# Later attentions: the first half's transposes of probabilities stand behind the queries' projection, and VectorE scales the rotation in front of their copy

## The reference

```python
def _layer(x, wqkv, qs, ksc, wo, lg, lb, w1, b1, w2, b2):
    h = shift_token(x)
    q, k, v = jnp.split(h @ wqkv, 3, axis=-1)          # 8 heads of 64
    q = l2norm(q) * qs
    k = l2norm(k) * ksc
    q, k = rotary_xpos(q, k)                           # q * cos * scale + rotate_half(q) * sin * scale
    o = local_attention(q, k, v)                       # windows of 128 queries see 256 keys
    x = x + o @ wo
    ...                                                # shift, layer norm, gated MLP, residual
for l in range(DEPTH):                                 # DEPTH = 2
    x = _layer(x, ...)
```

## Time and profile before

| | |
|---|---|
| median of 3 runs | 1796.6 us (1796.27 to 1797.61) |
| the profiled execution | 1796.15 us, of which 1794.4 us from the first to the last instruction |
| mean granted TensorE clock | 0.993 |
| busy: PE, DVE, ACT, POOL | 96%, 83%, 67%, 59% |
| chain that ended last: PE, DVE, ACT | 83%, 9%, 3% |

### The profile page before, as it was taken

The page is one execution under the profiler, slowest core; times in us unless marked ns, Lnnn a source line. Parts: engine busy times, 40 slices in busy tenths (PEclk is TensorE's granted clock), DMA queues, the critical chain, the costliest instruction groups (busy, mean ns, idle before and its releaser), DMA issues.

```text
span 1794.4 us, 43797 instructions
## 1 busy us (share of the span) xinstructions
PE 1730.8 (96%) x15424; PEld 1495.9 (83%) x15424; DVE 1495.9 (83%) x3797; ACT 1205.5 (67%) x3118; POOL 1066.2 (59%) x1030
## 2 busy tenths in 40 slices
PE   6999999999999999999999999989999999999997
PEld 4777777779998788888887888878888888888886
DVE  6999888858888898988987778789898888967776
ACT  6999999854445687877876344358787877743332
POOL 3666455534434778787774455377878777734343
PEclk9999999999999999999999999999999999999999
DMA  3111211022322111111112434321111111131221
GB/s 107 37 37 37 72 38 31 26 104 73 101 67 100 52 44 54 41 54 45 50 43 70 147 102 129 100 103 41 50 45 55 41 54 46 32 98 59 82 82 36
DMA packets 139813, 116.04 MB, mean 65 GB/s; under 512 B 10584, under 2 KB 138848, under 8 KB 138848
## 3 DMA queue, kind: packets, MB, share of 16 engines
q1 hardware_dynamic: 139616, 113.53, 20.4%
HBM read 75.74 MB, written 37.75 MB: 63 GB/s over the span
## 4 chain that ended last, share of the span: by engine, by line
PE 83%; DVE 9%; ACT 3%; issue 3%; POOL 1%; DMA 0%; SPq 0%; DVEq 0%; POOLq 0%; ACTq 0%
PE psum L567 17%; PE psum L569 17%; PE psum L568 17%; PE psum L908 6%; PE psum L876 5%; PE psum L889 5%; PE psum L682 3%; PE psum L664 3%; PE psum L850 3%; ACT a_probs L1720 2%; PE psum L922 2%; PE psum L617 1%; DVE a_neg_max L1211 1%; DVE psum L1209 1%; PE psum L654 1%
## 5 line engine op out<-in xcount | busy, mean ns | idle before, releaser
L1838 ACT ACTIVATE b_probs<-masked,neg_max 128x256 f32<-128x256 f32 (+1 forms) x512 | 250.1, 490 | 125.8 <-DVE neg_max L1345 125.8
L567 PE MATMUL psum<-wa_hi,b_h_hi 128*128 128x512 f32 (+1 forms) x576 | 232.6, 404 | 8.5 <-DVE wa_lo L1138 3.6
L1345 DVE CUSTOM_DVE_ANT_0 masked<-psum,mask 128x256 f32<-128x256 f32 (+1 forms) x512 | 177.3, 412 | 75.9 <-PE psum L876 75.9
L569 PE MATMUL psum<-wa_hi,b_h_lo 128*128 128x512 f32 (+1 forms) x576 | 213.4, 371 | 0.0
L568 PE MATMUL psum<-wa_lo,b_h_hi 128*128 128x512 f32 (+1 forms) x576 | 212.9, 370 | 0.0
L567 PE MATMUL psum<-g_h_hi,wm_hi 128*128 128x512 f32 (+1 forms) x480 | 190.4, 397 | 3.2 <-POOL g_h_lo L2107 1.6
L2056 POOL TENSOR_TENSOR g_in<-g_in,minus_half 128x16 f32<-128x16 f32 x64 | 188.2, 2940 | 4.5 <-DVE g_in L1297 4.5
L569 PE MATMUL psum<-g_h_hi,wm_lo 128*128 128x512 f32 (+1 forms) x480 | 189.2, 394 | 0.0
L568 PE MATMUL psum<-g_h_lo,wm_hi 128*128 128x512 f32 (+1 forms) x480 | 189.1, 394 | 0.0
L1460 POOL TENSOR_TENSOR g_in<-g_z,g_in 128x512 f32<-128x512 f32 x62 | 79.8, 1287 | 144.0 <-DVE g_in L1291 138.8
L1932 ACT ACTIVATE gate<-psum,vec_b 128x512 f32<-128x512 f32 x96 | 66.0, 688 | 146.7 <-PE psum L569 146.6
(11 more groups left out here) (168 smaller groups left out, 5613.1 us busy)
## 6 DMA issues: line engine op xcount, KB each, us to landing
x_mid<-y_out SPq DMA_DIRECT2D x96, 128.0 KB, 1.7
rope_in<-in_rope SPq DMA_DIRECT2D x64, 128.0 KB, 2.2
x_res<-x_state SPq DMA_DIRECT2D x64, 128.0 KB, 2.2
g_in<-x_mid SPq DMA_DIRECT2D x32, 256.0 KB, 3.6
g_old<-x_state SPq DMA_DIRECT2D x16, 512.0 KB, 4.0
out_x<-g_fin SPq DMA_DIRECT2D x15, 512.0 KB, 2.9
w_raw<-in_w_mlp_b SPq DMA_DIRECT2D x2, 2154.0 KB, 8.9
x_in<-in_x SPq DMA_DIRECT2D x32, 128.0 KB, 2.3
```

Source lines behind the costliest of these rows:

```text
L567: nc.tensor.matmul(out, a_hi, b_hi, start=first, stop=False)
L569: return nc.tensor.matmul(out, a_lo, b_hi, start=False, stop=last)
L1345: ins = nc.vector.tensor_tensor_reduce(out[:, at], src[:, at], (mask if now else mask0)[:, at], -1.0, BIG, ALU.add, ALU.min, neg_max[:, r, ...
L1838: ins = nc.scalar.activation(out, src, ACT.Exp, bias=neg_max[:, r, k:k + 1], scale=-1.0, accum_out=row_sum[:, n % 2, 4 * r + k:4 * r + k + 1])
```

## The change

In the loop of TensorE the transposes of the first half's probabilities move from in front of `project_q` to behind `transpose_x`, for every step that has them (at step 0 they stood there already). In the loop of VectorE `scale_rotated(s + 1)` moves in front of `copy_probs(s, 0)`. No instruction is added or removed.

```diff
@@ pe_attention
                 if b_chunk(s + 2) and s + 2 > 1:
                     project_k(s + 2)
-                if b_chunk(s) and s > 0:
-                    transpose_probs(s, 0)
                 if b_chunk(s + 2) and s + 2 > 1:
                     project_q(s + 2)
                 if b_chunk(s + 3) and s + 3 > 2:
                     transpose_x(s + 3)
-                if s == 0:
+                if b_chunk(s):
                     transpose_probs(s, 0)
@@ dve_attention
+                if b_chunk(s + 1) and s + 1 > 1:
+                    scale_rotated(s + 1)
                 if b_chunk(s):
                     copy_probs(s, 0)
-                if b_chunk(s + 1) and s + 1 > 1:
-                    scale_rotated(s + 1)
```

## The result

The changed kernel takes 1820.4 us (median of 4 runs, 1816.5 to 1821.6) against 1797.1 us for the kernel before on the same chip: the ratio is 1.013, with a 95% interval of 1.0117 to 1.0142. The forecast was 1819.8. The profiled execution took 1819.78 us against the 1819.3 that the sum had given for it, and its span is 23.6 us longer than before.

What follows compares the result with a forecast made beforehand. TensorE carries 83% of the chain, but VectorE's room in front of `h_low` was taken as 0.04 us. Longer steps sum to 23.2 us on 1796.15, 1819.3; with 0.45 for the median 1819.8 us, range 1810 to 1824.

Steps and rivals of the forecast that it cites:

- TensorE's sum: TensorE's work per step stays 12.57 us; first half's transposes start at 7.03 for 5.42, rotated parts' at 8.77.
- the saved change between products and transposes: Rival: on TensorE each of 56 steps could be 0.08 us shorter, 1791.0 us in all; chance 0.03.
- the fall of the clock: Rival: 26 transposes in a row drop TensorE to 1.2 GHz, 2.8 us more a step, near 1975 us; chance 0.02.
- An ordinary step, 12.94: Step without weight split: VectorE's first copy waits for transposes until 8.10, `h_low` ends at 11.27; 0.37 us over 12.57.
- The idle stretch of VectorE: VectorE would idle 0.3 to 0.5 us in front of the first copy in an ordinary step.
- A split step, 13.29: Step with a weight split on GpSimd: `tables` holds VectorE's scalings until 8.53, copy at 8.45; 0.64 us over 12.65.
- The room of VectorE, 0.04: VectorE can be only 0.04 us later in front of `h_low`; beyond it the step ends 1.67 us after `h_low`.
- The sum: Both attentions: 36 ordinary steps by 0.37, 13 split by 0.64, step 15 0.36, partly filled steps 1.2; together 23.2 us.
- the ten partly filled steps: Steps 1, 16, 17, 29, 30 of both attentions: each between -0.37 and +0.64, +0.12 us on average, 1.2 us for ten.
- TensorE's idle stretch in front of `project_v`: TensorE would idle about 0.3 us in front of `project_v` in every step.
- What was to become late next: Keys' rotated part, ready at 7.9 (8.53 in split steps) before TensorE wants it at 8.77; cover holds by 0.2 us.

Runs made afterwards that it cites:

- The spare instruction: Kernel before with one added VectorE sum over 128x512 into an unused tile, in front of the reciprocal in steps 2 to 28: 1822.6 us, ratio 1.0158.

## Why the prediction was right

- **TensorE's sum.** Right: transposes at 7.03, rotated parts' at 8.78, nothing else moved. The transposes, 26 in a row, keep 0.109 us each ((921.54 - 919.79) / 16, over the 16 of the probabilities), and the granted clock is 1.00 over both attentions, so neither the saved change between products and transposes nor the fall of the clock came about: the rotated parts' transposes still start at 8.78 for 8.77. The rule of the Trainium skill that was weighed there ("TensorE: Matmul & The Clock Gate", Part 4: transposes do not count as busy) has no effect that this trace shows.
- **An ordinary step, 12.94.** Measured 12.94 to 12.96. Copy at 8.10, `h_low` done at 11.28 for 11.27, next scores 1.67 behind. The idle stretch of VectorE is 0.21 where 0.3 was forecast; the scalings' record overlaps the rest. The parts are shown apart by experiments: 0.07 from VectorE's order, and 0.30 more with the late transposes, 0.22 of it when they move past the two token transposes.
- **A split step, 13.29.** Measured 13.24 to 13.29. The scalings end 1.16 behind `tables`, the very figure taken from the earlier trace rows; in all 50 full steps of the changed kernel it is 1.14 to 1.16. By the Trainium skill's rule ("SBUF — State Buffer", section "Who interferes with whom") read to the letter it would have been 1.28; the measurement decides for the shorter hold. That `tables` is the cause was shown by cutting it: 0.32 us of the 0.62 went. The other 0.30 stayed because the late transposes then hold the copy at 8.10, as in ordinary steps: each cause covers a part of the other.
- **The room of VectorE, 0.04.** The spare instruction gave 0.05. This number and the 1.67 us from `h_low` to the next scores, both read from one odd step of the trace before, carry the forecast together with the hold by `tables`. In step 15 it was GpSimd's L1460 that came late (9.54 for 9.25 in the same step of the first attention) and held the clamp; for the reading of the room this makes no difference.
- **The sum.** Forecast 23.2 us, measured 12.30 + 12.00 = 24.3 in the two attentions. The term that was mis-sized is that of the ten partly filled steps: 1.2 forecast, 1.93 measured (steps 1 of both attentions +0.48 and +0.18, 16 +0.19 and +0.20, 17 +0.73 and +0.72, 29 none, 30 -0.29 and -0.28). Step 17 has a weight split and took 13.27 like the others, but was shorter to begin with (12.54), and so lies above the +0.64 that was named as an upper bound. The remaining 50 steps gave 22.4 for 22.0. Outside the attentions the two traces differ by -0.8 us (start +0.3, end -1.1); the change does not reach there, and this is no part of its effect. That the forecast of 1819.8 lies within 0.6 us of the median is therefore partly luck: 1.1 us too little in the attentions stands against 0.8 us less outside, and the four runs themselves lie 5.1 us apart.
- **TensorE's idle stretch in front of `project_v`.** Forecast 0.3 in every step; the weight load of step 26 waits 0.29. `project_v` starts 0.26 later and takes 0.12 longer from its start to the next scores (1.61 for 1.49, by the rows above and the earlier trace rows), which adds up to the step's 0.38.
- **What was to become late next.** The rotated keys are ready at 7.89 and 8.51, and TensorE takes them up at 8.78, so that cover held.

Open: single steps are 0.3 us longer than their neighbours, step 28 of the first attention (12.88 before, 13.21 after) and step 15 of the second (12.93 and 13.55). With the clamp moved, in either kernel, both are gone. In the kernel before, step 28 loses its time between the clamp and the reciprocal (0.33 us), and step 15 by GpSimd's late L1460 (0.29 us). What starts either was not looked for.

## What to carry to other kernels

On an engine that works in order, find the instruction that another engine waits for and measure the room in front of it, from a step in which something happened to be late, before moving anything ahead of it: a busy share of 83% hid a room of 0.05 us. Moving work "behind" something costs what the in-order engine then waits, beyond its room: the last 0.22 us of it were paid one for one. And putting another instruction into the gap helps only if that one is ready and not held up itself. A tiny instruction that another engine can hold up belongs where nothing is awaited behind it, but its new neighbour on the other engine has to be looked at too, and so has the timetable of that engine: with shorter steps its own work comes later in the step.

## What the runs showed of the hardware

- A pair of VectorE instructions that read two SBUF inputs and started during GpSimd's `tables` ended at a fixed distance behind it, however long it had been held: 1.14 to 1.16 us in ordinary and split steps (1.82, 1.51 and 1.39 us long), for 1.28 us of its own. A single one ended 0.55 us behind GpSimd's L1136 (rows of step 7 with the clamp moved in the changed kernel), and 0.56 in the earlier trace rows.
- Not every GpSimd instruction holds VectorE up so: VectorE's first instruction of the rotation took 0.69 us in the middle of the power in step 26 of the kernel before (904.74, while the power ran from 903.35 to 906.26).
- The smallest instruction suffered most in proportion. The clamp, 128x16 and 0.17 us, took 0.28, 1.05 and 1.21 us, ending 0.03 to 0.04 behind GpSimd's 128x512 instruction each time.
- GpSimd is held up as well: its power on 128x16 takes 2.89 to 2.95 us, but 3.28 us and more in each of the 47 cases in which it started during a VectorE instruction with two SBUF inputs.
- A wait of TensorE is partly counted as busy: PE's busy time rose by 6.8 us in an attention with no matmul more. In step 26 the step grew by 0.38 us and the busy time by 0.30 (12.87 for 12.57). The product in front of the wait has a record of 0.28 us where the next one usually starts after 0.12, and the record of the first one behind the wait is 0.50 us for 0.40.
